# Scattering the routing records of a fused attention and mixture-of-experts kernel: eight tiles a step without landing waits in place of seven with them

## The reference

```python
def attn(x):                                    # x: 8 x 1024 x 256
    q, kv, a = split(rmsnorm(x) * gamma @ w_qkva.T, 3)
    a = sigmoid(a)
    y = scan over the tokens: y_t = a_t * y_(t-1) + kv_t
    return q * y

def ffn(x):                                     # 8 groups of 1024 tokens
    raw = softmax(x @ router_w)                 # 8 experts
    first and second choice of each token, position of the token
    among those of its group with this choice, dropped from 256 on
    expert_inputs = dispatch(x)                 # 8 experts x 2048 slots x 256
    hidden = gelu(expert_inputs @ w0[e]) * (expert_inputs @ w1[e])   # 1368 wide
    return combine(gates, hidden @ wo[e])

x = x + attn(layernorm(x))
x = x + ffn(layernorm(x))
```

## Time and profile before

| | before |
|---|---|
| median of three runs | 1708.48 us (1707.26 to 1712.23) |
| the profiled execution, its own time | 1707.26 us |
| its span, first to last instruction | 1705.5 us |
| mean granted TensorE clock | 0.991 |
| PE busy | 1661.1 us |
| DVE, ACT, POOL busy | 865.6, 725.2, 504.7 us |

### The profile page before, as it was taken

The page is one execution under the profiler, slowest core; times in us unless marked ns, Lnnn a source line. Parts: engine busy times, 40 slices in busy tenths (PEclk is TensorE's granted clock), DMA queues, the critical chain, the costliest instruction groups (busy, mean ns, idle before and its releaser), DMA issues.

```text
span 1705.5 us, 22844 instructions
## 1 busy us (share of the span) xinstructions
PE 1661.1 (97%) x8740; PEld 1435.4 (84%) x8740; DVE 865.6 (51%) x1825; ACT 725.2 (43%) x1327; POOL 504.7 (30%) x431
## 2 busy tenths in 40 slices
PE   7988989899999999999999999999999999999998
PEld 6877878788888888888888888888888888888887
DVE  7977854435544464446444644455444543464442
ACT  5756644334433453335333533344334433353332
POOL 2156665562222222222222222222222222222211
PEclk9989999999999999999999999999999999999999
DMA  7543221124211331115111511142113311241111
GB/s 164 159 119 114 83 80 56 15 36 103 51 26 25 81 70 25 20 25 119 22 23 23 121 26 26 26 109 41 26 25 91 60 26 26 52 94 20 22 13 13
DMA packets 124980, 96.21 MB, mean 56 GB/s; under 512 B 27144, under 2 KB 120776, under 8 KB 124872
## 3 DMA queue, kind: packets, MB, share of 16 engines
q1 hardware_dynamic: 96200, 60.66, 13.3%
q0 software_dynamic: 28672, 34.10, 12.7%
HBM read 60.11 MB, written 34.61 MB: 56 GB/s over the span
## 4 chain that ended last, share of the span: by engine, by line
PE 87%; DVE 4%; POOL 3%; DMA 2%; another core or an unknown queue 2%; issue 1%; ACT 1%; SPq 0%; DVEq 0%; POOLq 0%; ACTq 0%
PE bank L1533 27%; PE bank L1546 26%; PE bank L1562 17%; PE bank L1564 9%; PE bank L1359 4%; POOL slots L577 2%; PE bank L1439 2%; DMA slots<-records,sloti 1%; PE bank L1407 1%; PE bank L1557 1%; PE bank L1559 1%; DVE xring L929 0%; DVE st L936 0%; PE bank L1383 0%
## 5 line engine op out<-in xcount | busy, mean ns | idle before, releaser
L1298 DVE TENSOR_TENSOR y<-bank,sig 128x512 f32<-128x512 f32 (+1 forms) x352 | 242.9, 690 | 470.1 <-PE bank L1546 434.5
L649 POOL DMA_INDIRECT out<-xring,slot_records x128 | 215.1, 1680 | 897.1 <-DVE xring L1278 834.9
L1562 PE MATMUL bank<-wo,hhi 128*128 128x512 f32 (+1 forms) x1276 | 447.4, 388 | 0.0
L818 ACT ACTIVATE hhi<-y 128x512 fp32r<-128x512 f32 (+1 forms) x349 | 220.4, 632 | 522.4 <-DVE y L1298 490.3
L1564 PE MATMUL bank<-wo,hlo 128*128 128x256 f32 (+1 forms) x1396 | 382.1, 274 | 0.0
L1301 DVE TENSOR_TENSOR hlo<-y,hhi 128x512 fp32r<-128x512 f32 (+1 forms) x349 | 241.4, 692 | 243.4 <-ACT hhi L818 235.0
L808 ACT ACTIVATE sig<-bank 128x512 f32<-128x512 f32 (+1 forms) x352 | 208.9, 594 | 283.2 <-PE bank L1533 273.2
L1562 PEld LDWEIGHTS bank<-wo,hhi 128*128 128x128 f32 (+1 forms) x1276 | 239.2, 187 | 43.7 <-DVE hlo L1301 0.2
L1564 PEld LDWEIGHTS bank<-wo,hlo 128*128 128x128 f32 (+1 forms) x1396 | 261.9, 188 | 6.6
L1533 PE MATMUL bank<-xThi,whi 128*128 128x512 f32 x704 | 215.7, 388 | 4.7 <-ACT sig L808 4.2
L1546 PE MATMUL bank<-xThi,whi 128*128 128x512 f32 x704 | 212.6, 382 | 1.4 <-DVE y L1298 1.2
(11 more groups left out here) (133 smaller groups left out, 1572.2 us busy)
## 6 DMA issues: line engine op xcount, KB each, us to landing
stage<-in_L_ffn_w_kernel SPq DMA_DIRECT2D x160, 128.0 KB
stage<-in_L_ffn_wo_kernel SPq DMA_DIRECT2D x80, 128.0 KB
xring<-in_L_attn_x SPq DMA_DIRECT2D x16, 512.0 KB
out<-xring SPq DMA_DIRECT2D x16, 512.0 KB
x_rows<-rows SPq DMA_DIRECT2D x16, 512.0 KB
slots<-records,sloti POOLq DMA_INDIRECT x128
rows<-x_rows,slot_records POOLq DMA_INDIRECT x128
out<-xring,slot_records POOLq DMA_INDIRECT x128
```

What stands on the lines that cost most here:

```text
L649: pool.indirect_dma_start(out_rows, bass.IndirectOffsetOnAxis(idx, 0), ysb[:, t % 2, j, :], None, compute_op=ALU.add).then_inc(added, 16)
L818: act.activation(h_high(e, t, hc)[0:n, :], hf[0:n, hc % 2, :], ACT.Copy).then_inc(h_hi, 1)
L1298: dve.tensor_tensor(hf[0:n, hc % 2, :], up_value(e, t, hc)[0:n, :], gel[0:n, hc % 2, :], ALU.mult).then_inc(mul_done, 1)
L1562: pe.matmul(lines(yb[j][:, :]), high, lines(wo[0:n, hc, :, :].rearrange("p s c -> p (s c)")), start=hc == 0, stop=end, skip_group_check=True)
```

## The change

The landing waits are removed (`landed` and the wait behind `gather(0, 1)`). `scatter` now takes a group and a range of its tiles; it waits for the emptied table and for `routed` whenever the range begins at tile 0. A step scatters 8 tiles: tile 2 of group i-3 first, then `powers1`, `powers2(.,0)`, tiles 3 to 6 of group i-3, `powers2(.,1)`, tile 7 of group i-3, and tiles 0 and 1 of group i-2. Behind the pipeline, the six tiles left of group 5 are scattered in one call, ahead of both `powers2` of the last group. The number of scatters is the same, 128. Other engines' programs are unchanged.

```diff
-            def landed(n):
-                g, t = divmod(n, TILES)
-                pool.wait_ge(scattered[t // HT][g % 2], SCATTERED * (g // 2) + 16 * 2 * (t % HT + 1))
-
-            def scatter(a, b):
-                for n in range(a, b):
-                    g, t = Turn(n // TILES), n % TILES
-                    if n == 0:
-                        pool.wait_ge(emptied, 16 * 2 * FT)
-                    elif (n - a) % 2 == 0:
-                        landed(n - 1)
-                    if t == 0:
-                        wait(pool, routed, g, 1, 1)
+            def scatter(g, a, b):
+                if a == 0:
+                    pool.wait_ge(emptied, 16 * 2 * FT)
+                    wait(pool, routed, g, 1, 1)
+                for t in range(a, b):
                     for k in range(2):
                         pool.indirect_dma_start(
...
-            FIRST, PER_STEP = 2, TILES - 1
-
             def step(i):
-                A, C = (live(i, n) for n in (1, -1))
-                n = FIRST + PER_STEP * (i.value - 3)
+                A, C, Dg, late = (live(i, n) for n in (1, -1, -2, -3))
                 if i.value == -2:
                     pool.wait_ge(consts_made, 1)
-                if n > 0:
-                    scatter(n, n + 2)
+                if late:
+                    scatter(i.plus(-3), SCATTER_SPLIT, SCATTER_SPLIT + 1)
                 if A:
                     powers1(i.plus(1))
                 if i.value == G - 1:
                     gather(0, 0)
                 if C:
                     powers2(i.plus(-1), 0)
-                if n > 0:
-                    scatter(n + 2, n + 6)
+                if late:
+                    scatter(i.plus(-3), SCATTER_SPLIT + 1, TILES - 1)
                 if C:
                     powers2(i.plus(-1), 1)
-                if n > 0:
-                    scatter(n + 6, n + 7)
-                elif i.value == 2:
-                    scatter(0, FIRST)
+                if late:
+                    scatter(i.plus(-3), TILES - 1, TILES)
+                if Dg:
+                    scatter(i.plus(-2), 0, SCATTER_SPLIT)
 
             pipeline(step)
 
-            left = FIRST + PER_STEP * (G - 3)
-            last_late = TILES * (G - 2)
-            landed(left - 1)
             gather(0, 1)
-            pool.wait_ge(rows_loaded[1], 16 * FJ)
-            scatter(left, last_late - 5)
+            scatter(Turn(G - 3), SCATTER_SPLIT, TILES)
             powers2(last_group, 0)
-            scatter(last_late - 5, last_late - 2)
             powers2(last_group, 1)
-            scatter(last_late - 2, last_late)
```

More of the change, by code:

```diff
@@ L30 @@
 NORM_MIN = 1e-12
+SCATTER_SPLIT = 2
 FREE_MUL = 2
@@ L643, in expert @@
                     if (e, t) == (0, 0):
-                        scatter(TILES * (G - 2), TILES * (G - 1))
+                        scatter(before_last, 0, TILES)
                     for j in range(FJ):
@@ L654, in expert @@
                     if (e, t) == (0, 0):
-                        scatter(TILES * (G - 1), TILES * G)
+                        scatter(last_group, 0, TILES)
             experts(pool, expert)
```

## The result

The changed kernel takes 1757.38 us (median, 1751.19 to 1764.84) against 1707.87 us (1706.50 to 1712.23) for the kernel before, measured side by side: a ratio of 1.0286, 95% interval 1.0253 to 1.0319. It is 49.5 us slower; the forecast was 15 us faster. The profiled execution took 1761.3 us.

A forecast was written before the change was run, and what follows sets the result against it. PE bounds the expert stage, but from 88 to 151 us waits through DVE for POOL's powers, queued behind scatters and landing waits. Terms -9.7, -1.6, -4.4, +1.2, -1.2 sum to -15.7 us: 1693 us against 1708.48, range 1684 to 1706.

The forecast's parts named there:

- Taking it away frees POOL without a queue growing behind it: POOL's scatters: the landing wait is latency, not a limit on how many fit; 40.6 us in 23 waits.
- waits that no engine explains: Rival: scatters in flight cause DVE's waits of unknown releaser (15.9 us); half as much again, +8 us, 1701 us; chance 0.08.
- slower: Rival: POOL blocks behind a full descriptor queue, each issue costing 2.35 us; +45 us over five steps, 1754 us; chance 0.08.
- Steps 1 to 3: Pipeline's steps 3 and 4: earlier powers remove PE's 6.88 and 2.51 us gaps, shorten the 2.30 one; -9.7, -1.6, -4.4 us.
- step 3: Pipeline step: `powers2(2,0)` comes 7.4 us earlier, PE's 6.88 us gap goes and its clock gains; -9.7 us.
- Step 4: Pipeline's steps 5 to 7: 16 issues a step and a loop slightly longer than PE's work; +1.2 us, bounds 0 and +4.
- the new loop: Steps 5 to 7: DVE's `factors2` to `routed`, then POOL's six issues and powers; 26.0 us against PE's 25.4 to 25.7.
- Step 5: Behind the pipeline: `gather(0,3)` comes 5.3 us earlier, so PE's 1.15 us wait for it goes; -1.2 us.

The follow-up runs named there:

- depth: Changed kernel plus a wait, ahead of tile n, for the scatters of tile n-3 (at most six in flight): 1675.03 us, ratio 0.9884, in a quiet set.
- affected sets: Groups of kernels run side by side on one chip; the kernel before took 1701 to 1709 us, traces show DVE or ACT waits of unknown releaser.
- pause_2: Changed kernel plus an unread POOL power (about 1.3 us) ahead of every second tile, no landing wait: 1711.97 us, ratio 1.0061, in an affected set.
- long_pause_2: Kernel before, its scatter landing waits replaced by 1.3 us POOL powers, both waits around `gather(0, 1)` removed: 1699.75 us, ratio 0.9951, affected set.
- depth_2: The kernel of depth run again, against the kernel before in an affected set: 1752.84 us, ratio 1.0280.
- quiet set: Group of kernels run side by side on one chip; the kernel before took 1694 us, no trace shows DVE or ACT waits of unknown releaser.

## Why the prediction was wrong

**"Taking it away frees POOL without a queue growing behind it"** is the step that failed. It put the effect on PE, ACT and DVE at nothing; the runs showed 72 to 82 us in its place. As to the DMA queue it held: scatter issues stayed at 0.96 us (the median), and the limit on scatters in flight in `depth` changed nothing. But the step took the landing wait for latency only. It was also a break in POOL's issuing, and where breaks are missing, in the affected sets, DVE and ACT wait up to 15 us for what PE has finished. That these breaks let the signals through is shown by `pause_2` and `long_pause_2`, which wait for no scatter's landing.

**The rival "waits that no engine explains"** named the thing and mis-sized it: +8 us on the forecast, where the measured time lies 64 us above the forecast. Two readings went into that size. It added up 15.9 us of DVE's waits, where DVE's were 26.5 us in all and DVE's and ACT's together 35.5 us. And it took them to grow by half; they grew fourfold, as the pipeline's runs of mostly four issues became runs of mostly six and eight, and the longest run of all went from eight to 24. Its "against" (DVE has none from 88 to 151 us) was true of a kernel in which breaks stood after every four issues; it said nothing of one without them. Its condition, scatters in flight, is refuted by `depth_2`.

**The rival "slower"** gave 1754 us, near the measured 1757, by another mechanism: issues of 2.35 us behind a full queue. There are none: the longest scatter issue of the affected trace takes 1.76 us. That it hit the time is chance.

**Steps 1 to 3** (-15.7 us). In the affected trace step 3 did start as forecast: DVE's wait for `powers2` at 99.25 us is over at 92.13 us, and PE's gap of 6.88 us has gone. Behind it new gaps of 5.03 us (107.86) and 2.92 us (141.86) opened, each behind a wait of ACT's for PE's signal that began during a run of eight issues. In the quiet trace the steps came out closely: `factors2` at 92.05, 118.61 and 144.26 us after waits of 1.33 us each, where 92, 119 and 1.2 us were forecast, and the second one of a step at 129.75 us where 131 was forecast; the granted clock 1.00 from 88 to 151 us; no PE gap of over 1.1 us from 60 to 230 us.

**Step 4** (+1.2 us). In the quiet trace the markers of `transpose_back` are 26.0, 26.6, 25.7 and 25.7 us apart (90.88, 116.90, 143.49, 169.14, 194.79 us), 26.0 on average, so the new loop costs no more than said. **Step 5** can't be told apart from the rest in the affected trace; in the quiet one PE is full to 0.1 us from 330 to 420 us, and no wait at the gathered rows of about 1 us is left there.

**The sum** was -15.7 us; in the quiet set -19.4 us was measured (1694.45 to 1675.05). Counted from the kernel before, the range (2 to 24 us faster) takes that in, so the steps hold where the effect is absent. The first comparison fell in an affected set. Its trace of before carried the sign, 35.5 us of waits without a releaser beside POOL's runs, and the earlier trace rows showed its largest line.

**What stays open.** Which path PE's signals and POOL's issues share, and what makes a set quiet or affected. The runs show neither; that the signals are held, and not the end of the matmuls later than recorded, is read from the records and not tested. The record has a span and a granted clock for every execution, so all were traced in some way; that the tracing itself has a part in the effect isn't excluded. It wasn't tried whether longer runs of gathers or accumulates alone do it.

Two pages of the Trainium skill bear on this without settling it. "Perfetto Trace Analysis", DMA Instruction — SWDGE (GPSIMD), says that such an instruction is shown as ending when POOL has finished generating its descriptors, not when the data has moved. The traces agree in so far as a gather's issue takes 0.95 us and the gather lands after 2.8 us. By that page POOL writes descriptors for 0.96 us of every 1.26 us of an unbroken run. "DMA: Bandwidth & Descriptors", Latency and other measured facts, offers as a guess that the fetching of these descriptors crowds some ports of SBUF, to explain two slower DMA engines. Whether PE's signals meet such traffic no run here shows.

## What to carry to other kernels

A wait that looks like pure latency may also keep an engine's instruction stream from being unbroken; before removing it, see what the other engines do during the longest run without it, and add up the waits without a releaser over all engines, not for one. Where POOL issues indirect DMAs in long rows beside PE, cut the rows: breaks of 1.6 us, mostly after four issues, kept this kernel at 1699 us in both sorts of set, where it took 1675 or 1757 us without. A gain seen in one set of runs is not yet a gain; a kernel whose time hangs on such an effect has to be compared in several.

## What the runs showed of the hardware

- Unbroken indirect DMA issues of POOL (0.96 us, every 1.26 us) go along with waits for PE's signals of up to 15 us on DVE and ACT, in some sets of runs; in others the same 24 in a row cause none. The same kernel takes 1675 or 1757 us.
- Most of these waits that end outside a run end 0.8 to 1.3 us behind its last issue (13 of 17); 11 of 28 end inside a run.
- Breaks of 1.57 us, mostly after four issues, all but end it (6.2 us of waits left of 144.6), breaks of 0.80 us halve it (61 to 75 us), and a power of 1.3 us in the break does at least as well as a wait for a landed scatter (3 to 6 us left, against 20 to 36).
- Beside them, the time from issue to landing is given on the page of every quiet run (2.8 us for a gather, 3.9 us for an accumulate) and on those of the affected runs only once (3.8 us for an accumulate, in `pause_2`): the trace couldn't assign it elsewhere. It may belong to the same thing; nothing here tells.
